# Selective-scan and expert kernel: second spread in the head, in-projection and dt product placed later, output product in two steps, two norm buffers

## The reference

```
xn  = layernorm(x)
out = x + attn(xn) + ffn(xn)

def attn(x):                      # two selective scans, one forwards, one backwards in time
    n  = layernorm(x) * g + b
    of = mamba(n);  ob = mamba(n reversed) reversed
    return concat(of, ob) @ combine_w.T + combine_b + x

def mamba(x):                     # 256 channels, 16 states each, 512 steps
    xi, z = split(x @ in_w.T)
    xi = silu(conv4(xi) + conv_b)
    dt, B, C = split(xi @ x_w.T)              # 8, 16, 16 columns
    delta = softplus(dt @ dt_w.T + dt_b)
    h[t] = h[t-1] * exp(delta[t] * A) + delta[t] * xi[t] * B[t]
    y = sum over states of h * C + xi * D
    return (y * silu(z)) @ out_w.T

def ffn(x):                       # 8 experts, the largest router logit picks one
    e = argmax(x @ router_w.T)
    return (silu(x @ gate_w[e].T) * (x @ up_w[e].T)) @ down_w[e].T
```

## Time and profile before

| | |
|---|---|
| median of 3 runs | 925.07 us |
| lowest, highest | 924.85, 928.36 us |
| span of the profiled execution | 921.1 us |
| instructions in the span | 10735 |
| VectorE busy | 882.0 us, 96% |
| GpSimd busy | 801.1 us, 87% |
| TensorE busy | 736.6 us, 80% |
| ScalarE busy | 699.8 us, 76% |

### The profile page before, as it was taken

How to read it: one execution, slowest core, us unless ns; L and a number is a source line. 1 busy time by engine, 2 the same in 40 slices (tenths; PEclk the granted TensorE clock), 3 DMA queues, 4 the chain that set the end, 5 groups by cost and what they waited for, 6 DMA issues and landing times. The chain is left out here.

```text
span 921.1 us, 10735 instructions
## 1 busy us (share of the span) xinstructions
PE 736.6 (80%) x3033; PEld 327.7 (36%) x3033; DVE 882.0 (96%) x631; ACT 699.8 (76%) x1183; POOL 801.1 (87%) x450
## 2 busy tenths in 40 slices
PE   8678877777488978979788987979786987878377
PEld 5233322231134534444343534436332431323022
DVE  5899999999899999999999999999999999999986
ACT  5798876646569789888989889998979776585531
POOL 1578786999999989998799898999798989999994
PEclk9978789788698999999999999989999799879578
DMA  7875342343265546445365636455554345553300
GB/s 229 224 221 144 109 111 58 139 100 101 110 162 158 152 154 175 138 136 149 134 151 177 156 84 209 124 185 125 181 140 134 85 95 163 108 170 75 85 0 12
DMA packets 87227, 123.45 MB, mean 134 GB/s; under 512 B 7929, under 2 KB 58490, under 8 KB 83202
## 3 DMA queue, kind: packets, MB, share of 16 engines
q1 hardware_dynamic: 85122, 118.58, 46.5%
q0 software_dynamic: 2048, 4.20, 1.5%
HBM read 75.44 MB, written 14.29 MB: 97 GB/s over the span
## 5 line engine op out<-in xcount | busy, mean ns | idle before, releaser
L1360 POOL TENSOR_TENSOR hs<-hs,C_rep 128x1024 f32<-128x1024 f32 x250 | 585.5, 2362 | 52.1 <-DVE hs L1150 27.8
L947 ACT ACTIVATE dA<-delta_rep,A_sb 128x511 f32<-128x511 f32 x512 | 338.2, 717 | 92.8 <-DVE hs L1150 47.1
L1131 DVE TENSOR_TENSOR in_b<-in_b,B_rep 128x1024 f32<-128x1024 f32 x256 | 300.1, 1216 | 15.7 <-PE in_b L589 14.7
L1150 DVE TENSOR_TENSOR_SCAN hs<-dA,in_b 128x1024 f32<-128x1024 f32 x128 | 285.3, 2267 | 5.3 <-PE y L623 5.3
L1148 DVE TENSOR_TENSOR_SCAN hs<-dA,in_b 128x1024 f32<-128x1024 f32 x128 | 285.1, 2267 | 1.4 <-PE y L623 1.4
L589 PE MATMUL in_b<-du,cst 128*128 128x512 f32 x256 | 160.8, 714 | 57.3 <-DVE hs L1150 43.6
L623 PE MATMUL y<-hs,cst 128*32 128x512 f32 x1024 | 139.5, 652 | 21.9 <-POOL hs L1360 21.9
L550 PE MATMUL front<-xpad,w_in 128*128 128x512 f32 x248 | 119.3, 616 | 9.0 <-ACT xi L876 7.3
L956 ACT ACT_TABLE_LOAD x71 | 91.1, 1283 | 8.3 <-PE moe L733 3.7
L589 PEld LDWEIGHTS in_b<-du,cst 128*128 128x128 f32 x256 | 46.8, 214 | 134.4 <-issue 132.6
L623 PEld LDWEIGHTS y<-hs,cst 128*32 128x32 f32 x1024 | 29.6, 116 | 113.8 <-issue 71.0
(11 more groups left out here) (147 smaller groups left out, 803.0 us busy)
## 6 DMA issues: line engine op xcount, KB each, us to landing
delta_rep<-tmpA SPq DMA_DIRECT2D x126, 256.0 KB, 3.9
C_rep<-dbc_scratch SPq DMA_DIRECT2D x16, 1024.0 KB, 7.2
B_rep<-dbc_scratch SPq DMA_DIRECT2D x15, 1024.0 KB, 5.0
gu_w<-in_gate_up SPq DMA_DIRECT2D x39, 384.0 KB, 3.8
dn_w<-in_down SPq DMA_DIRECT2D x39, 192.0 KB, 2.6
xs<-sorted_tokens SPq DMA_DIRECT2D x39, 64.0 KB, 3.9
sorted_ffn<-ys SPq DMA_DIRECT2D x39, 64.0 KB, 2.4
sorted_tokens<-up_f SPq DMA_DIRECT2D x9, 256.0 KB, 4.5
```

Source lines behind the costliest of these rows:

```text
L947: i = e.activation(dA[:, m % NA, r * L + 1:(r + 1) * L], src, ACT.Exp, scale=A_sb[:, d, 2 * p + jj, RH * rh + r:RH * rh + r + 1])
L1131: e.tensor_tensor(to, in_b[:, 2 + 2 * odd, :].unsqueeze(1).broadcast_to([P, RH, L]), by, ALU.mult).then_inc(dve_mult, 1)
L1150: e.tensor_tensor_scan(to[:, ::-1], a[:, 1:n + 1][:, ::-1], b[:, ::-1], 0.0, ALU.mult, ALU.add).then_inc(dve_scan, 1)
L1360: e.tensor_tensor(hs[:, m % NH, :], hs[:, m % NH, :], C_rep[:, u % 2, RH * rh:RH * rh + RH, :].rearrange("p r t -> p (r t)"), ALU.mult).th ...
```

## The change

Seven edits:

1. `spread_du(0, 1)`, the spread for the pair 2 and 3, stands in the head behind `first_pair(1)` and no longer in step 1.
2. `in_proj(1, 1)`, the second half of the projection of unit 1, stands in step 3 behind the spread of that step (which is the third one); before, its two parts were in steps 2 and 3 ahead of it.
3. On ScalarE the two `keep_z` of unit 0 stand behind `decay(2)`, before they stood ahead of it.
4. `dt_proj(v, 1)` of odd units from 3 on goes from step 16 v - 10 to 16 v - 9, where it stands behind the spread of that step.
5. Of the output product of batches 0 to 6, q = 0 and 1 are one step earlier than q = 2 and 3. Before, all four were in one step.
6. `xn` has two buffers, with a semaphore each for the store; `norm_one(c)` waits for the store and the turn of c - 2.
7. The scratch area of the indirect DMAs is 4096 bytes a partition. Before, the constructor's own value was taken.

```diff
-        return s0 + NSTEP + (12, 12, 12, 12, 10, 13, 13, 12)[k]
+        return s0 + NSTEP + (11, 11, 12, 12, 10, 13, 13, 12)[k]
...
-        xn = sb("xn", [P, KB, H])
+        xn = sb("xn", [P, 2, KB, H])
...
-                e.dma_start(by_batch(xn_d, c), xn[:, :, :]).then_inc(out_xn, 16)
+                e.dma_start(by_batch(xn_d, c), xn[:, c % 2, :, :]).then_inc(out_xn[c % 2], 16)
...
             first_pair(1)
+            spread_du(0, 1)
             first_skip()
...
                 for v in fronts(m, -14, -14):
-                    in_proj(v, 1, 0)
+                    if v > 1:
+                        in_proj(v, 1, 0)
                 for v in fronts(m, -13, -13):
-                    in_proj(v, 1, 1)
+                    if v > 1:
+                        in_proj(v, 1, 1)
...
-                if m % 2 and m + 1 < LAST:
+                if m % 2 and m > 1 and m + 1 < LAST:
                     v, k = divmod(m + 1, NSTEP)
                     spread_du(v, k // 2)
+                for v in fronts(m, -13, -13):
+                    if v == 1:
+                        in_proj(v, 1, 0)
+                        in_proj(v, 1, 1)
...
-                for v in fronts(m, -9, -10):
+                for v in fronts(m, -9, -9):
                     dt_proj(v, 1)
...
-                if c:
-                    e.wait_ge(out_xn, 16 * c)
-                    e.wait_ge(pe_xn_turned, c)
-                normalize(xn, xin[:, c % 2, :, :], c, 0, act_xn)
+                if c >= 2:
+                    e.wait_ge(out_xn[c % 2], 16 * (c // 2))
+                    e.wait_ge(pe_xn_turned, c - 1)
+                normalize(xn[:, c % 2, :, :], xin[:, c % 2, :, :], c, 0, act_xn)
...
-                if m == 0:
-                    keep_z(0, 0)
-                    keep_z(0, 1)
...
                 if m + LEAD < LAST:
                     table(EXP_SET)
                     decay(m + LEAD)
+                if m == 0:
+                    keep_z(0, 0)
+                    keep_z(0, 1)
...
-    nc = bacc.Bacc("TRN2", target_bir_lowering=False, num_devices=1)
+    nc = bacc.Bacc("TRN2", target_bir_lowering=False, num_devices=1,
+                   dynamic_dma_scratch_size=4096)
```

More of the change, by code:

```diff
@@ L199, in mamba_moe_kernel @@
         xin = attn_in
-        late_in = (xn[:, :, :], attn_in[:, 0, :, :])
+        late_in = (xn[:, 0, :, :], attn_in[:, 0, :, :])
         logits = sb("logits", [P, NBLK, E])
@@ L246, in mamba_moe_kernel @@
         in_x = sems("in_x", 2)
-        out_xn = sem("out_xn")
+        out_xn = sems("out_xn", 2)
         in_again = sem("in_again")
@@ L454, in sync_program @@
                     if R0 + 5 + 20 * c // 8 == m:
-                        e.wait_ge(out_xn, 16 * (c + 1))
+                        e.wait_ge(out_xn[c % 2], 16 * (c // 2 + 1))
                         if c >= 2:
@@ L509, in turn_xn @@
                 for k in range(KB):
-                    i = e.transpose(M[:, k * P:(k + 1) * P], xn[:, k, :], ident)
+                    i = e.transpose(M[:, k * P:(k + 1) * P], xn[:, c % 2, k, :], ident)
                 i.then_inc(pe_xn_turned, 1)
@@ L1325, in gpsimd_program @@
                     elif i == 0:
-                        e.wait_ge(out_xn, 16 * NB)
+                        for k in range(2):
+                            e.wait_ge(out_xn[k], 8 * NB)
                         e.wait_ge(pe_xn_turned, NB)
```

## The result

| | before | after |
|---|---|---|
| median of 5 runs each, same chip | 924.85 us | 914.44 us |
| lowest, highest | 922.67, 928.36 | 911.08, 918.21 |
| profiled execution | span 921.1 | time 917.37, span 915.4 |
| VectorE busy | 882.0 | 881.2 |
| TensorE busy | 736.6 | 741.9 |

The ratio of the two is 0.9896, with a 95% interval of 0.9871 to 0.992. In us that is -9.6 (-11.9 to -7.4); 8.4 had been forecast. The profiled execution of after happens to be one of the long ones: 917.37 for a median of 914.44. The two profiles lie only 5.7 us apart in their spans, so they show a part of the 9.6.

A forecast was written before the change was run, and what follows sets the result against it. VectorE's unchanged work plus its 39.1 us of idle time was taken as the bound. Terms -3.4 - 3.0 - 2.0 + 0 + 0 = -8.4 us gave a span of 912.7, plus 4.0 around it: 916.7 us, range 914.0 to 921.5.

The forecast's parts named there:

- What bounds it: Whole kernel: VectorE's work, left alone by the change, sets the time; only its waits, within 39.1 us idle, can shrink.
- Head, -3.4: Head, pair 2 and 3: the second spread moved ahead removes VectorE's 3.41 us wait, worth -3.4 us.
- buffers, -3.0: Head, ScalarE's normalization: two buffers remove 10.3 us of its idle time; VectorE gains 3.0 us, ends 0 and 3.5.
- its own rival: Head: ScalarE is no earlier, VectorE reaches step 6 when it did, 3.9 us are void: 920.6 us; chance 15%.
- the decay of step 6: Head, ScalarE: it ended 0.17 us before its scan; needed at least 3.7 us earlier, 4.5 expected, margin 0.8.
- 2.8 us of cover: Head: the third spread ends at 35.9 us, VectorE comes at 38.7, so it is hidden by 2.8 us.
- The dt product, -2.0: Units 11 and 13: second dt product behind the spread removes VectorE's 0.66 and 1.34 us waits; between 0 and -2.0.
- The output product, 0: Output products of batches 0 to 6: splitting takes the same wait earlier, value 0; ends -3.2 and +12 us.
- The rival by which its waits also go: Output products: the split also removes their waits, as TensorE used to wait there; -3.2 us more, 913.5 us; chance 12%.
- The scratch area, 0: GpSimd's 64 indirect DMAs: the smaller area costs 0, worst end 54 us; scatters keep 1.0 us; cost rival's chance 8%.
- Around the span: Outside the profiled span: 4.0 us, median 925.07 less span 921.1, added to the forecast span of 912.7.
- What would show it: Signs in the profile: named waits gone, VectorE runs through from 25 us, batch 1 keeps 1.83 us, scatters keep 1.0 us.

The follow-up runs named there:

- x_head: Kernel before plus only the head edits: early second spread, later second half of unit 1's projection, z copies behind the third decay. Ratio 1.0004, +0.4 us.
- z_e1norm: Kernel before plus the early second spread, two norm buffers and smaller scratch area, without moving the projection half or z copies. Ratio 0.9963, -3.4 us.
- y_nosplit: Kernel before plus all edits except the output product in two steps. Ratio 0.9875, -11.6 us, median 914.93 us.
- y_headnorm: Kernel before plus the three head edits, two norm buffers and smaller scratch area; dt product and output product unchanged. Ratio 0.9935, -6.0 us.
- z_dt_two: Kernel before with the second dt product moved behind the spread at units 11 and 13 only. Ratio 0.9972, -2.6 us.
- x_dt: Kernel before with only the second dt product of odd units moved behind the spread. Ratio 0.9950, -4.6 us.
- x_outp: Kernel before with only the output product split over two steps. Ratio 1.0005, +0.5 us.
- y_ring: Kernel before with only the indirect DMAs' scratch area set to 4096 bytes. Ratio 0.9987, -1.2 us.
- z_dt_rest: Kernel before with the second dt product moved behind the spread at units 3, 5, 7, 9 and 15 only. Ratio 1.0001, +0.1 us.
- x_norm: Kernel before with only two norm buffers and the smaller scratch area. Ratio 0.9980, -1.9 us.
- y_all: All seven edits measured again, against the kernel before. Ratio 0.9863, -12.7 us, median 913.36 us.
- z_more_c: All seven edits, plus the products with C of steps 49 and 207 on VectorE instead of GpSimd, against the kernel before. Ratio 0.9885, median 911.98 us.

## Why the prediction was right, and where its sizes were not

916.7 us had been forecast, 8.4 less than the median shown. Measured was a ratio that means 9.6 less, and 12.7 less when taken again; of the medians, 914.44 lies in the range that began at 914.0, and 913.36 just below it. By its parts:

- **What bounds it.** Right: VectorE's busy time did not move (882.0 and 881.2), only its waits.
- **Head, -3.4, and buffers, -3.0.** Their sum, 6.4, was right: 6.0. Priced one by one they were wrong in the way that they were written down. Alone the head gives nothing and the buffers 1.9. The prediction said of the buffers that "this edit also carries the first one", and by its own rival, in which ScalarE isn't earlier, 3.9 us are void. x_head is that rival made real. With both edits in, the sum was right and its terms were not: by the profiles the wait at the pair 2 and 3 is worth 4.4 us in the mean, and the other waits fell by 1.3 (3.05 to 1.75). The 3.4 came from an execution with one of the shortest of these waits, the 3.0 took nearly all of the others to go; the two errors cancel. The prediction named the decay of step 6 as the late one, though; what VectorE waited for was the spread behind the router's matmuls.
- **Edits 2 and 3.** They were priced with the head at 2.8 us of cover. The cover was 2.3, and z_e1norm shows what it is made of: without these edits the third spread is 1.49 us late.
- **The dt product, -2.0, bounds 0 and -2.0.** Mis-sized: -4.6 (-6.8 to -2.5) alone, and -5.4 by the medians of y_nosplit and y_headnorm. The failed step was to take the two waits of one execution as the price, and their sum as an upper bound. The wait of 1.34 is in all eight executions without the edit, but that at unit 11 is between nothing and 1.30, and what else VectorE lost in these stretches wasn't counted: together they are 3.0 us, and z_dt_two gives 2.6. That leaves 1.6 to 2.0 of the 4.6; the intervals overlap, and where the rest comes from stays open. The other units by themselves measured +0.1, and a faster clock over the whole program it isn't either: the mean granted clock of the 12 runs of x_dt is 0.889, that of the 35 beside them 0.892.
- **The output product, 0.** Right, and in the manner forecast: the same wait, taken as one or two. The rival by which its waits also go (913.5 us) would have fit the time as well; x_outp speaks against it, since alone the edit gave +0.5 us and no more than -2.1 by its interval, and all seven edits without this one give 914.93.
- **The scratch area, 0.** Right: 1007 ns before and after, and 0.9987 alone (its interval holds -3.1 to +0.7 us). The Trainium skill (SBUF — State Buffer, SBUF size: 192, 224, or 256?) says that the descriptors lie in this area; that a smaller one would cost time it does not say, and here it didn't.
- **Around the span.** 4.0 us had been taken. In every run that has both, the time less the span is 1.8 to 2.2 (917.37 less 915.4; 915.39 less 913.5; 912.59 less 910.6). The 4.0 set one execution's span beside the median of others. It cancels in the difference, but it means that the profiled execution of before took about 923.1 us, 2 us less than the median.
- **What would show it.** The signs came true but for one: no wait at the pair 2 and 3, none ahead of `norm_one`, 0.89 for 5.20 us at the router, none at units 11 and 13, one wait as two at batch 1, 1007 ns. VectorE did not run through from 25 us: 2.3 us of waits are left from 54 to 69. And the last sign but one says little, since the wait at batch 1 comes and goes with the execution.

So the mechanisms held. The total owes something to luck: the term of the dt product was too small by 1 to 3 us, the head was right as a sum of two wrong terms, and the measurement itself is uncertain by more than 2 us.

## What to carry to other kernels

Two waits that follow each other within a few us on the busiest engine may have one cause or two, and an edit may give nothing alone and its full price together with another. Write down for each edit which resource is late next and when, and price such edits as a set. A wait on an engine in strict order is caused by what stands ahead in its queue: follow the named releaser back, here spread, router, copy, `norm_one`, store, before you decide what to move. And don't take the waits in one profiled execution as an upper bound on what can be won: read two or three executions, and count a wait only if it is in most of them. Where the same wait and the same slow matmuls stand in every execution without an edit and in none with it, that shows a cause that medians within 2 us of each other can't.

## What was not expected of the hardware

Equal instructions in equal order find TensorE at another clock from one execution to the next, and this moves waits of 1 to 5 us about in the program. The first pair of rows is from the kernel after, unit 7, the first dt product and the spread, both on the slow side (the VectorE row is the wait that follows):

```profile
441.57 2.07 PE L582 MATMUL front<-tmpB,w_dt 8*128 8x512 f32 x2 [0.91 <-ACT tmpB L905]
443.57 2.08 PE L589 MATMUL in_b<-du,cst 128*128 128x512 f32 x2
...
445.69 2.36 DVE L1138 TENSOR_TENSOR in_b<-in_b,B_rep 128x1024 f32<-128x1024 f32 x2 [1.54 <-PE in_b L589]
```

The same two in the kernel before:

```profile
445.32 1.12 PE L582 MATMUL front<-tmpB,w_dt 8*128 8x512 f32 x2 [1.95 <-ACT tmpB L898]
446.37 1.12 PE L589 MATMUL in_b<-du,cst 128*128 128x512 f32 x2
```

2.07 and 2.08 us against 1.12 and 1.12, and a wait of 1.54 us that before doesn't have. This is the 300 to 600 us stretch in which after lost 2.4 us. Before had waited longer (1.95 for 0.91) ahead of these rows and was nonetheless at the fast clock, so it is not the last wait alone that decides.

In the head, where x_outp, y_ring and z_dt_two are the same as before in this stretch, the wait ahead of the pair 2 and 3 was 5.40, 5.37 and 5.24 us, where the earlier trace rows show 3.41 (3.82 and 3.26 in x_dt and z_dt_rest). For 30 to 36 us the kernel before had a granted clock of 1.00 and y_ring this:

```profile
30.00:36.00 6.00, 4.82 (x7) 2.00 (x8) 3.03 (x2) 5.21 (x11) 5.92 (x4) 0.72 0.59 117
```

And the wait at the output product of batch 1 is there in 6 of the 14 profiled executions (before 1.83 us, after 1.86, x_norm 0.71, y_all 1.58, z_e1norm 0.83, z_more_c 1.02) and absent in 8, whatever edits they have. The kernel before takes 917.73 to 929.62 us over 35 runs, 1.3%. Its faster runs are on the whole those with the higher mean granted clock: in the three groups 0.01 more goes with 3.8, 4.1 and 5.8 us less, with correlations of -0.57, -0.60 and -0.88. With 12 runs against 35 the interval is still 2 us to either side (x_norm), so an edit worth 2 us can just be told from none. A single trace doesn't tell a wait that is always there (1.34 us at unit 13, in all eight without edit 4) from one that comes and goes.

The Trainium skill (TensorE: Matmul & The Clock Gate, What's actually happening) says that the number of slow matmuls differs from run to run of the same kernel, and puts the penalty of the start below 1% of a typical span. The variation is borne out by the rows above, here in the middle of the program and not at its start alone. The run times spread by 1.3%, of which the clock is a part that no run sets apart, and that is more than any single edit of this change brings.
